# A fused attention and mixture-of-experts layer on one core: a shorter loop body in a branch that is not taken, and one unit's loads issued later

## The chip, the core and the metric

One Trainium2 chip, one core of it. The metric is device time in microseconds (us) from one launch. The engines are named as in the profile: PE (TensorE matmul), PEld (its weight load), DVE (VectorE), ACT (ScalarE), POOL (GpSimd) and SP (SyncE, which issues nearly all transfers). A "q" behind an engine's name is its sequencer or its queue of transfers.

## What is computed

The reference, cut to what matters (B = 4, T = 1024, C = 256, 16 heads of 16; all float32):

```
att = einsum('bhqd,bhkd->bhqk', q, k) / sqrt(D) + rel_bias      # causal mask, then softmax over keys
y   = einsum('bhqk,bhkd->bhqd', softmax(att), v) @ W_proj.T + b_proj
x   = layernorm(x + y)
e   = argmax(x @ gate_w.T)                                      # each token goes to one of 2 experts
out = layernorm(x + relu(x @ w1[e] + b1[e]) @ w2[e] + b2[e] + relu(x @ sw1 + sb1) @ sw2 + sb2)
```

The kernel does not subtract an exact row maximum before each exponential. It computes a bound (the "guard") from the norms of queries and keys and feeds its negative in as two extra rows of the query operand. Only if that bound is too loose (the flag `wide`) does it compute exact row maxima. With the inputs of this reference the flag is 0, so that part is built into the program but is skipped at run time.

## The kernel before, in words

Three stages run one after the other: `project_in` (queries, keys and values from x), `attend` (attention), `feed_forward` (projection, gate, experts, shared network). Between the first two stands `exact_maxima`, whose code on SP, PE and DVE lies inside an `If` on the flag `wide`. Each engine has its own instruction stream and the engines meet through semaphores only.

**The end of `project_in`.** DVE computes the flag and the guard value in a chain of one-element operations (L620 to L636). PE spreads the guard over the partitions (L742), ACT writes it to `neg_guard` (L528), and POOL fills `guard_fill` from it (L488, L490) and signals `ready.fill`. SP's stream at that place is the list that the change reorders. It stores tile 6's projected queries and keys to DRAM (`qk_d`, L412). It loads the second attention unit's stacks, which is `first_stack(1)`: eight transfers into `k_st` and `q_second` (L252 to L255), 1.5 MB together. It waits for `ready.fill`, writes the guard rows of all later units to DRAM (`guard_d`, L446 and L448), waits for those writes, loads the second unit's guard rows (L272), waits for `ready.decided`, and stores the last tile (L412).

**The branch.** On DVE the `If` stands at L801. Its body has a loop over batches (L810) and in it a loop over the two halves of the heads (L811), whose body is written out for 8 heads times 8 blocks of queries, 64 pairs of an addition (L822) and a maximum (L826). Behind the body come L836, which signals `ready.decided`, and the attention's code. PE's and SP's branches stand at L840 and L776.

**`attend`.** A unit is four heads of one batch, so there are 16 units. A unit has 9 steps times 2 pairs of heads, 18 in all. For each, PE computes scores into one of three slots of PSUM (L1157), DVE adds the bias in place for blocks near the diagonal (L1123), ACT takes the exponential (L1068 in the first unit, L1066 later) into `probs`, and PE multiplies by the values into `o_ps` (L1176). PE computes scores two steps ahead. Units take turns between two buffers: `q_first` for the first and third, `q_second` for the second and fourth. PE waits for a unit's ten loads before its first score (`st_ld`, L1146). SP loads the third unit once the last tile has been stored (L967) and PE has made all scores of the first unit (L933).

Of the kernel before, what the change touches and what calls it, by code (L numbers as in the profile page):

```python
# [14 lines left out]
ALU = mybir.AluOpType  # L15
ACT = mybir.ActivationFunctionType
AX = mybir.AxisListType

P = 128
B, T, C = 4, 1024, 256  # L20
H, D = 16, 16
HID = 1024
E = 2
KC = C // P
# [7 lines left out]
KB = T // P  # L32
BUCKETS = 32
WIN = 2 * P
# [212 lines left out]
def load_parts(sp, q_rows, k_rows, first, k_st, q_st, loaded):  # L247

    for side in range(2):
        at = ROWS_H * side  # L250
        heads = slice(first + side, first + side + UH - 1, 2)
        sp.dma_start(k_st[at:at + 2 * D].bitcast(F32), k_rows[0:2 * D, heads]).then_inc(loaded, 16)  # L252
        sp.dma_start(k_st[at + 2 * D:at + 3 * D].bitcast(F32), k_rows[0:D, heads]).then_inc(loaded, 16)
        sp.dma_start(q_st[at:at + D].bitcast(F32), q_rows[0:D, heads]).then_inc(loaded, 16)
        sp.dma_start(q_st[at + D:at + 3 * D].bitcast(F32), q_rows[0:2 * D, heads]).then_inc(loaded, 16)  # L255


def unit_rows(qk_d, b, g):

    rows = qk_d.rearrange("b c n (d h) t -> b c (n d) h t", d=D)  # L260
    q_rows = rows[bass.ds(b, 1), g // 2].rearrange("o r h t -> (o r) h t")
    k_rows = rows[bass.ds(b, 1), KC + g // 2].rearrange("o r h t -> (o r) h t")
    return q_rows, k_rows, UH * (g % 2)


def load_guard(sp, guard_d, b, g, q_st, loaded):

    rows = guard_d[bass.ds(b, 1)].rearrange("o g h t -> (o g) h t")
    for side in range(2):
        at = ROWS_H * side + STACK  # L270
        heads = slice(UH * g + side, UH * g + side + UH - 1, 2)
        sp.dma_start(q_st[at:at + GUARD].bitcast(F32), rows[:, heads]).then_inc(loaded, 16)  # L272
# [9 lines left out]
def overlay(nc, name, shape, dt, at):  # L282
    return nc.alloc_sbuf_tensor_at(name, shape, dt, offset=at)
# [21 lines left out]
def project_in(nc, keep, ready, slots, o_ps, ident, wp_hi, wp_lo, bp_row, v_all, shared_at, y_at, bias_t, wide, neg_guard, guard_fill, qk_d, guard_d, pad_row, rs_at,  # L305
# [3 lines left out]
    HG = H // KC  # L309
    with ExitStack() as ctx:  # L310
# [68 lines left out]
        def sync(sp):  # L379
# [47 lines left out]
            def first_stack(g):  # L427

                q_st = (q_first, q_second)[g]
                load_parts(sp, *unit_rows(qk_d, 0, g), k_st[:, g], q_st, st_ld[g])  # L430
                if g < AP_UNITS:
                    load_guard(sp, guard_d, 0, g, q_st, st_ld[g])
# [6 lines left out]
            sp.wait_ge(guard_out, 16)  # L439
            first_stack(0)  # L440
            body(B - 1, True, False)
            first_stack(1)
            sp.wait_ge(ready.fill, 2)
            for part in range(GUARD):
                src = guard_fill[:, part].bitcast(F32)
                sp.dma_start(guard_d[0, part, AP_UNITS * UH:H].rearrange("h t -> (h t)").rearrange("(p n) -> p n", p=P),  # L446
                             src[:, 0:(H - AP_UNITS * UH) * T // P]).then_inc(ready.guard_rows, 16)
                sp.dma_start(guard_d[1:B, part].rearrange("b h t -> b (h t)").rearrange("b (p n) -> p b n", p=P),  # L448
                             src.unsqueeze(1).to_broadcast([P, B - 1, P])).then_inc(ready.guard_rows, 16)
            sp.wait_ge(ready.guard_rows, 32 * GUARD)  # L450
            load_guard(sp, guard_d, 0, AP_UNITS, q_second, st_ld[AP_UNITS])
            sp.wait_ge(ready.decided, 1)
# [290 lines left out]


        return Stage(sync, gpsimd, scalar, vector, tensor)


def exact_maxima(nc, keep, ready, slots, o_ps, ident, bias_t, wide, qk_d, guard_d, q_first, q_second, st_ld, shared_at):


    HG = H // KC
    STEPS_C = HG * KB
    PARTS_DMAS = 8
    with ExitStack() as ctx:
        def sb(name, shape, dt=F32):
            return ctx.enter_context(nc.sbuf_tensor(name, shape, dt))

        def sem(name):
            return keep.enter_context(nc.semaphore(name))

        bias_q = overlay(nc, "bias_q", [P, H, WIN], F32, shared_at)
        q_all = overlay(nc, "q_all", [P, UH // 2, T], F32R, shared_at + 4 * H * WIN)
        k_all = overlay(nc, "k_all", [P, UH // 2, T], F32R, shared_at + 4 * H * WIN + 2 * UH * T)
        most = sb("most", [P, H * KB])
# [4 lines left out]
        added = sem("added"); maxed = sem("maxed"); most_ps = sem("most_ps"); neg_ok = sem("neg_ok")  # L769
# [29 lines left out]
        def vector(dve):  # L799
            dve.wait_ge(ready.wide, 1)  # L800
            with dve.If(dve.value_load(wide[:, :], min_val=0, max_val=1) != 0):  # L801
                dve.sem_inc(ready.decided, 1)
                dve.sem_inc(maxed, 2)
                dve.sem_inc(neg_ok, 1)
                for i in range(H // UH):
                    dve.wait_ge(turned, i + 1)
                    dve.tensor_copy(bias_q[:, UH * i:UH * i + UH, :],
                                    slots[:, i % 2].rearrange("p a (i x) -> p (a i) x", x=WIN)).then_inc(bias_q_ok, 1)
                dve.wait_ge(bias_q_ok, H // UH)
                with dve.Fori(0, B) as b:  # L810
                    with dve.Fori(0, KC) as c:  # L811
                        for h in range(HG):
                            for qb in range(KB):
                                k = KB * h + qb
                                n = STEPS_C * (KC * b + c) + k
                                row = slots[:, k % 2].rearrange("p a x -> p (a x)")
                                first = P * max(qb - 1, 0)
                                width = P * (qb + 1) - first
                                dve.wait_ge(scored, n + 2)
                                if k == 0:  # L820
                                    dve.wait_ge(neg_ok, b + 1)
                                dve.tensor_tensor(row[:, first:first + width], row[:, first:first + width],  # L822
                                                  bias_q[:, bass.ds(c * HG + h, 1), WIN - width:WIN].rearrange("p o x -> p (o x)"),
                                                  ALU.add).then_inc(added, 1)
                                dve.wait_ge(added, n + 1)
                                dve.tensor_reduce(most[:, bass.ds(c * STEPS_C + k, 1)], row[:, 0:P * (qb + 1)],  # L826
                                                  AX.X, ALU.max).then_inc(maxed, 1)
                    dve.wait_ge(most_ps, b + 1)
                    dve.tensor_scalar(neg[:, :], o_ps[:, 0, 0:P], -1.0, None, ALU.mult).then_inc(neg_ok, 1)
                    dve.wait_ge(neg_ok, b + 2)  # L830
                    dve.wait_ge(neg_out, 16 * GUARD * (b + 1))
                    dve.tensor_copy(neg_parts[:, 0], neg[:, :]).then_inc(split, 1)
                    dve.wait_ge(split, GUARD * b + 1)
                    dve.tensor_tensor(neg_parts[:, 1], neg[:, :], neg_parts[:, 0].bitcast(F32), ALU.subtract).then_inc(split, 1)
                dve.wait_ge(neg_out, 16 * GUARD * (B + 1))
            dve.sem_inc(ready.decided, 1)  # L836
# [40 lines left out]


        return Stage(sync, idle, idle, vector, tensor)


# [1249 lines left out]
```

## Time and profile before

| what | value |
|---|---|
| time, median of 3 runs | 818.05 us (817.14 to 818.75) |
| profiled execution, first to last instruction | 820.4 us |
| PE busy | 779.3 us, 95% of the span |
| ACT busy | 541.0 us, 66% |
| DVE busy | 509.0 us, 62% |
| POOL busy | 240.7 us, 29% |
| mean granted TensorE clock | 0.977 of full speed |

The busy share is an average over stages with different limits. Beside the span no other time of the profiled execution is given; it is 2.35 us above the median of the runs.

### The profile page before, as it was taken

To read this page: it belongs to the slowest core of one execution; us is meant where nothing else is said; L and a number is where in the kernel's file an instruction comes from. 1 tells how busy PE (TensorE), PEld (TensorE's weight loads), DVE (VectorE), ACT (ScalarE), POOL (GpSimd) and SP (SyncE) were. 2 spreads that over 40 slices of the span, in tenths; PEclk is the share of its full clock that TensorE was granted. 3 is DMA by queue.
4 is the path that set the end of the run, shared out by engine and by line. 5 is a ranking of instruction groups with operands and counts; after the bars stand their busy time and mean duration, and the time that the engine had idled before them with its cause. 6 is when DMAs were issued, how large, how long until landed. Compare 5 with 4: busy or idle time off the path is not lost.

```text
span 820.4 us, 16215 instructions
## 1 busy us (share of the span) xinstructions
PE 779.3 (95%) x6153; PEld 568.7 (69%) x6153; DVE 509.0 (62%) x1118; ACT 541.0 (66%) x700; POOL 240.7 (29%) x200
## 2 busy tenths in 40 slices
PE   7998849999999999999999999999999999999993
PEld 6886524444444444444889989889899998999992
DVE  4666426667666666765877788976634545554543
ACT  5666449999999999998455555544444455555442
POOL 6224310000020022036243545252532333223332
PEclk9999959999999999999999999999999999999997
DMA  8899975667797799891681211110475433444300
GB/s 238 231 287 279 216 173 93 93 120 120 118 179 129 122 156 177 136 174 20 119 285 59 66 65 54 53 45 34 145 264 198 161 123 140 168 176 165 141 27 29
DMA packets 57929, 114.41 MB, mean 139 GB/s; under 512 B 8019, under 2 KB 35064, under 8 KB 55544
## 3 DMA queue, kind: packets, MB, share of 16 engines
q1 hardware_dynamic: 53048, 100.60, 52.4%
q0 software_dynamic: 4800, 12.73, 4.4%
q8 instruction: 50, 0.82, 0.5%
q14 instruction: 31, 0.25, 0.1%
HBM read 57.75 MB, written 32.49 MB: 110 GB/s over the span
## 4 chain that ended last, share of the span: by engine, by line
PE 84%; DVE 6%; ACT 4%; issue 4%; DMA 1%; POOLq 0%; DVEq 0%; POOL 0%; ACTq 0%
PE slots L2043 20%; PE o_ps L1176 15%; PE slots L1157 14%; PE slots L2060 11%; PE o_ps L2060 10%; PE slots L708 6%; PE o_ps L670 2%; PE slots L1406 2%; ACT probs L1066 2%; DVE slots L1123 1%; PE slots L648 1%; PE slots L2025 1%; ACT probs L1068 1%; DVE junk L1798 1%; DVE other_row L1875 1%
## 5 line engine op out<-in xcount | busy, mean ns | idle before, releaser
L1066 ACT ACTIVATE probs<-slots 128x1024 f32<-128x1024 f32 x270 | 254.1, 1033 | 1.6
L1123 DVE TENSOR_TENSOR slots<-slots,bias_t 128x512 f32<-128x512 f32 (+1 forms) x288 | 163.6, 607 | 100.8 <-PE slots L1157 86.0
L1949 DVE TENSOR_TENSOR h_lo<-h_f,h_hi 128x512 fp32r<-128x512 f32 (+1 forms) x136 | 96.6, 712 | 107.6 <-PE o_ps L2060 70.1
L1176 PE MATMUL o_ps<-probs,v_st 128*32 128x384 f32 (+3 forms) x1920 | 155.5, 433 | 0.3 <-ACT probs L1066 0.3
L1767 ACT ACTIVATE h_f<-slots,b_cur 128x512 f32<-128x512 f32 (+1 forms) x72 | 47.9, 665 | 88.1 <-PE slots L2043 87.8
L1767 ACT ACTIVATE h_f<-slots,b_c 128x512 f32<-128x512 f32 x64 | 43.9, 687 | 67.6 <-PE slots L2043 65.6
L1771 ACT ACTIVATE h_hi<-h_f 128x512 fp32r<-128x512 f32 (+1 forms) x136 | 84.3, 620 | 4.3
L1157 PEld LDWEIGHTS slots<-q_first,k_st 50*128 50x128 f32 x480 | 38.7, 191 | 68.4 <-ACT probs L1066 37.2
L1157 PE MATMUL slots<-q_first,k_st 50*128 50x128 f32 (+3 forms) x480 | 70.0, 377 | 14.5 <-ACT probs L1068 12.5
L1176 PEld LDWEIGHTS o_ps<-probs,v_st 128*32 128x32 f32 x1920 | 46.5, 109 | 44.7 <-issue 28.0
L1157 PEld LDWEIGHTS slots<-q_second,k_st 50*128 50x128 f32 x480 | 37.5, 184 | 53.6 <-ACT probs L1066 42.2
L1157 PE MATMUL slots<-q_second,k_st 50*128 50x128 f32 (+3 forms) x480 | 68.7, 369 | 0.8
L1722 POOL DMA_INDIRECT out<-o_out,id_i x32 | 35.6, 1113 | 102.6 <-DVE o_out L1913 95.3
L1005 POOL COPY v_st<-v_all 128x512 f32<-128x512 f32 x16 | 9.7, 617 | 173.4 <-PE o_ps L1176 173.4
L1684 POOL DMA_INDIRECT xs_d<-x,slot_i x32 | 35.9, 1122 | 74.5 <-DVE slot_i L1829 67.2
L1684 POOL DMA_INDIRECT base_d<-base,slot_i x32 | 40.7, 1273 | 46.6 <-DVE base L1891 38.9
L2043 PE MATMUL slots<-x1t_lo,cur_hi 128*128 128x512 f32 (+1 forms) x144 | 43.3, 382 | 0.0
L2043 PE MATMUL slots<-x1t_hi,cur_lo 128*128 128x512 f32 (+1 forms) x144 | 43.3, 382 | 0.0
L2043 PE MATMUL slots<-x1t_hi,cur_hi 128*128 128x512 f32 (+1 forms) x144 | 43.2, 381 | 0.0
L2043 PE MATMUL slots<-x1t_hi,shared_hi 128*128 128x512 f32 x128 | 41.4, 404 | 1.2 <-ACT x1t_hi L1336 1.2
L2060 PE MATMUL slots<-experts_hi,h_hi 128*128 x144 | 41.3, 287 | 0.2
L2043 PE MATMUL slots<-x1t_lo,shared_hi 128*128 128x512 f32 x128 | 40.7, 399 | 0.2 <-DVE x1t_lo L1398 0.2
(243 smaller groups left out, 1709.3 us busy)
## 6 DMA issues: line engine op xcount, KB each, us to landing
qk_d<-parts SPq DMA_DIRECT2D x32, 512.0 KB, 8.3
cur_hi<-experts_hi SPq DMA_DIRECT2D x9, 1024.0 KB, 4.8
cur_lo<-experts_lo SPq DMA_DIRECT2D x9, 1024.0 KB, 6.9
k_st<-qk_d SPq DMA_DIRECT2D x32, 256.0 KB
xs_sb<-xs_d SPq DMA_DIRECT2D x8, 528.0 KB, 4.7
x_in<-L_attn_x SPq DMA_DIRECT2D x8, 512.0 KB, 7.8
k_st<-qk_d SPq DMA_DIRECT2D x32, 128.0 KB
q_first<-qk_d SPq DMA_DIRECT2D x16, 256.0 KB
```

The costliest lines, as they stand in the source:

```text
L708: ins = pe.matmul(slots[:, 1 + c // 2, c % 2], wq[w][:, kc, P * c:P * c + P], xt[a][:, t, kc, :], start=(i == 0 and kc == 0), stop=(i == 2 ...
L1066: nc.scalar.activation(dst, src, ACT.Exp).then_inc(exped, 1)
L1123: ins = dve.tensor_tensor(tile, tile, bias_t[:, h0:h0 + 2, first:first + w], ALU.add)
L1157: ins = pe.matmul(slots[:, k % SLOTS, h, col:col + w], k_st[at:at + KROWS, buf, pair, P * j:P * j + P], q_st[buf][at:at + KROWS, pair, q0: ...
L1176: ins = pe.matmul(o_ps[32 * j2:32 * j2 + 2 * D, half, q:q + w], v_st[:, g, j, j2, :], probs[:, (k + j2 // 2) % PBUFS, j2 % 2, col:col + w] ...
L1684: pool.indirect_dma_start(rows[:, :], bass.IndirectOffsetOnAxis(slot_i[:, t % 2, k:k + 1], 0), src[:, k, :], None).then_inc(done, 16)
L1722: pool.indirect_dma_start(out_rows[:, :], bass.IndirectOffsetOnAxis(id_i[:, j % 2, k:k + 1], 0), (o_out if j < EXP_TILES - 1 else y2)[:, k ...
L1767: nc.scalar.activation(h_f[:, q % 2, 0:w], l1_bank[q % 2][:, 0:w], ACT.Relu, bias=bias).then_inc(hf_ok, 1)
L1771: nc.scalar.activation(h_hi[:, n % 3, 0:w], h_f[:, q % 2, 0:w], ACT.Copy).then_inc(hh_ok, 1)
L1949: dve.tensor_tensor(h_lo[:, n % 3, 0:w], h_f[:, q % 2, 0:w], h_hi[:, n % 3, 0:w].bitcast(F32), ALU.subtract).then_inc(hl_ok, 1)
L2043: ins = pe.matmul(l1_bank[q % 2][:, 0:P * blocks(u)], w1_of(u, w)[:, kc, P * q:P * q + P], (xt_hi, xt_lo)[a][:, kc, 0:P * blocks(u)], star ...
L2060: ins = pe.matmul(acc_bank[k], (h_hi, h_lo)[a][:, n % 3, P * k:P * k + P], w2_chunk(u, w, q, e), start=(q == 0 and i == 0), stop=(q == HC ...
```

## The change

Two places of the program are rewritten, and nothing that is computed changes.

First, in the part of `exact_maxima` that DVE skips, the two nested loops (two halves of the heads, and eight heads written out in each) become one loop over all 16 heads. The body is then written out for one head: 8 pairs of addition and maximum in place of 64. Second, in SP's stream of `project_in`, `first_stack(1)` is moved from before the wait for `ready.fill` to behind the four writes of the guard rows.

```diff
             first_stack(0)
             body(B - 1, True, False)
-            first_stack(1)
             sp.wait_ge(ready.fill, 2)
             for part in range(GUARD):
...
                 sp.dma_start(guard_d[1:B, part].rearrange("b h t -> b (h t)").rearrange("b (p n) -> p b n", p=P),
                              src.unsqueeze(1).to_broadcast([P, B - 1, P])).then_inc(ready.guard_rows, 16)
+            first_stack(1)
             sp.wait_ge(ready.guard_rows, 32 * GUARD)
             load_guard(sp, guard_d, 0, AP_UNITS, q_second, st_ld[AP_UNITS])
             sp.wait_ge(ready.decided, 1)
...
                 with dve.Fori(0, B) as b:
-                    with dve.Fori(0, KC) as c:
-                        for h in range(HG):
-                            for qb in range(KB):
-                                k = KB * h + qb
-                                n = STEPS_C * (KC * b + c) + k
-                                row = slots[:, k % 2].rearrange("p a x -> p (a x)")
...
+                    with dve.Fori(0, H) as h:
+                        for qb in range(KB):
+                            n = H * KB * b + KB * h + qb
+                            row = slots[:, qb % 2].rearrange("p a x -> p (a x)")
...
+                            dve.tensor_reduce(most[:, bass.ds(KB * h + qb, 1)], row[:, 0:P * (qb + 1)],
+                                              AX.X, ALU.max).then_inc(maxed, 1)
```

On DVE, at the branch around the exact maxima, the rows of the instruction stream before are these (each with its number in the stream; L801 is the `If`, L1123 the first bias addition of the attention):

```order
75 L801 TENSOR_LOAD wide
76 L801 ISA x2
77 L801 COMPARE_AND_BRANCH
78 L807 COPY bias_q<-slots 128x1024 x4
...
363 L834 TENSOR_TENSOR neg_parts<-neg,neg_parts 128x128
364 L810 REGISTER_ALU
365 L810 COMPARE_AND_BRANCH
366 L801 UNCONDITIONAL_BRANCH
367 L1123 TENSOR_TENSOR slots<-slots,bias_t 128x2x128 x2
```

The same place of DVE's stream in the changed kernel (L1123 has become L1121):

```order
75 L801 TENSOR_LOAD wide
76 L801 ISA x2
77 L801 COMPARE_AND_BRANCH
78 L807 COPY bias_q<-slots 128x1024 x4
...
125 L832 TENSOR_TENSOR neg_parts<-neg,neg_parts 128x128
126 L810 REGISTER_ALU
127 L810 COMPARE_AND_BRANCH
128 L801 UNCONDITIONAL_BRANCH
129 L1121 TENSOR_TENSOR slots<-slots,bias_t 128x2x128 x2
```

The branch keeps its place, and the instruction that it lands on moves from row 367 to row 129: 289 rows are jumped over before, 51 after. DVE's whole stream shrinks from 883 rows to 645, and everything behind the branch lies 238 rows nearer the start.

On SP, at the end of `project_in`, the rows before (tile 6's stores, then the second unit's stacks, the guard rows, and the last tile's stores):

```order
L412 DMA qk_d<-parts 128x2x512 x4
L252 DMA k_st<-qk_d 32x2x1024
...
L255 DMA q_second<-qk_d 32x2x1024
L446 DMA guard_d<-guard_fill 128x96
L448 DMA guard_d<-guard_fill 128x3x128
L446 DMA guard_d<-guard_fill 128x96
L448 DMA guard_d<-guard_fill 128x3x128
L272 DMA q_second<-guard_d 2x2x1024 x2
L412 DMA qk_d<-parts 128x2x512 x4
```

And the same place of SP's stream in the changed kernel (L446 and L448 have become L445 and L447):

```order
L412 DMA qk_d<-parts 128x2x512 x4
L445 DMA guard_d<-guard_fill 128x96
L447 DMA guard_d<-guard_fill 128x3x128
L445 DMA guard_d<-guard_fill 128x96
L447 DMA guard_d<-guard_fill 128x3x128
L252 DMA k_st<-qk_d 32x2x1024
...
L255 DMA q_second<-qk_d 32x2x1024
L272 DMA q_second<-guard_d 2x2x1024 x2
L412 DMA qk_d<-parts 128x2x512 x4
```

The eight stack loads (the "..." stands for six of them) have changed places with the four writes of guard rows. The loads of the second unit's guard rows and the last tile's stores stay behind both.

## Rows read from the trace of the kernel before

**Rows 1.** The page's head, and busy time, share of span, instructions of PE.

```profile
span 820.4 us, 16215 instructions
...
PE 779.3 (95%) x6153; PEld 568.7 (69%) x6153; DVE 509.0 (62%) x1118; ACT 541.0 (66%) x700; POOL 240.7 (29%) x200
```

**Rows 2.** Stretches: PE, PEld, DVE, ACT, POOL busy (x), PEclk, DMA share, GB/s.

```profile
98.00:100.50 2.50, 1.42 (x9) 0.85 (x8) 0.02 (x1) 1.20 (x3) 1.70 (x4) 1.00 1.19 235
100.50:112.50 12.00, 0.00 (x0) 0.00 (x0) 1.36 (x3) 1.09 (x2) 4.14 (x6) 0.50 1.00 132
112.50:120.00 7.50, 7.11 (x34) 2.61 (x34) 2.86 (x5) 6.19 (x8) 0.00 (x0) 0.50 0.68 248
120.00:122.00 2.00, 2.00 (x28) 1.31 (x24) 0.87 (x2) 1.10 (x2) 0.00 (x0) 0.73 0.42 159
134.00:151.00 17.00, 16.85 (x184) 7.61 (x180) 11.30 (x21) 16.87 (x19) 0.62 (x1) 1.00 0.68 111
```

**Rows 3.** Chain that ended last, 98 to 132 us: start, us, what.

```profile
98.97 11.73 issue
110.70 0.02 DVEq L836
...
110.88 0.45 DVE slots L1123
...
111.41 3.13 ACT probs L1068 x3
```

**Rows 4.** Transfer queues, whole span: packets, MB, share of 16 engines.

```profile
q8 instruction: 50, 0.82, 0.5%
q14 instruction: 31, 0.25, 0.1%
```

**Rows 5.** The same queues, 99 to 107 us: the data queue q1.

```profile
q1 hardware_dynamic: 429, 1.17, 107.7%
```

**Rows 6.** The same queues, 107 to 109 us: the instruction queue q14.

```profile
q14 instruction: 1, 0.01, 2.0%
```

**Rows 7.** Timeline of PE, 97 to 99.6 us, first score: start, us.

```profile
99.45 0.50 PE L1157 MATMUL slots<-q_first,k_st 50*128 50x512 f32 x2 [1.00 <-ACT neg_guard L528]
```

**Rows 8.** Timeline of PE, 97 to 150 us: second and third unit's first scores.

```profile
130.55 1.02 PE L1157 MATMUL slots<-q_second,k_st 50*128 50x512 f32 x4
...
147.83 0.84 PE L1157 MATMUL slots<-q_first,k_st 50*128 50x512 f32 x4
```

**Rows 9.** Timeline of ACT, 95 to 133 us: first unit's 18 exponentials.

```profile
111.41 6.14 ACT L1068 ACTIVATE probs<-slots,neg_guard 128x1024 f32<-128x1024 f32 x6 [11.83 <-DVE slots L1123]
118.85 2.12 ACT L1068 ACTIVATE probs<-slots,neg_guard 128x1024 f32<-128x1024 f32 x2 [1.31 <-DVE slots L1123]
121.87 10.15 ACT L1068 ACTIVATE probs<-slots,neg_guard 128x1024 f32<-128x1024 f32 x10 [0.90 <-DVE slots L1123]
```

**Rows 10.** Timeline of SP's issues, 84 to 136 us: start, us.

```profile
89.17 0.50 SPq L252 DMA_DIRECT2D k_st<-qk_d  x1
...
99.52 0.37 SPq L446 DMA_DIRECT2D guard_d<-guard_fill  x1
...
100.94 0.47 SPq L448 DMA_DIRECT2D guard_d<-guard_fill  x1
113.61 0.58 SPq L272 DMA_DIRECT2D q_second<-guard_d  x2
114.30 3.32 SPq L412 DMA_DIRECT2D qk_d<-parts  x4
129.72 0.35 SPq L252 DMA_DIRECT2D k_st<-qk_d  x1
```

**Rows 11.** Stretches again, by transfers (columns as in Rows 2).

```profile
114.50:121.50 7.00, 6.91 (x40) 2.89 (x44) 2.53 (x5) 5.17 (x6) 0.00 (x0) 0.53 0.83 303
...
129.70:142.70 13.00, 12.83 (x138) 5.54 (x133) 7.95 (x15) 12.88 (x15) 0.62 (x1) 1.00 0.88 146
142.70:147.00 4.30, 4.30 (x48) 2.07 (x52) 3.56 (x7) 4.29 (x5) 0.00 (x0) 1.00 0.02 5
```

More of the change, by code:

```diff
@@ L810, in vector @@
                 with dve.Fori(0, B) as b:
-                    with dve.Fori(0, KC) as c:
-                        for h in range(HG):
-                            for qb in range(KB):
-                                k = KB * h + qb
-                                n = STEPS_C * (KC * b + c) + k
-                                row = slots[:, k % 2].rearrange("p a x -> p (a x)")
[L817 to L827, printed above, removed]
+                    with dve.Fori(0, H) as h:
+                        for qb in range(KB):
+                            n = H * KB * b + KB * h + qb
+                            row = slots[:, qb % 2].rearrange("p a x -> p (a x)")
+                            first = P * max(qb - 1, 0)
+                            width = P * (qb + 1) - first
+                            dve.wait_ge(scored, n + 2)
+                            if qb == 0:
+                                dve.wait_ge(neg_ok, b + 1)
+                            dve.tensor_tensor(row[:, first:first + width], row[:, first:first + width],
+                                              bias_q[:, bass.ds(h, 1), WIN - width:WIN].rearrange("p o x -> p (o x)"),
+                                              ALU.add).then_inc(added, 1)
+                            dve.wait_ge(added, n + 1)
+                            dve.tensor_reduce(most[:, bass.ds(KB * h + qb, 1)], row[:, 0:P * (qb + 1)],
+                                              AX.X, ALU.max).then_inc(maxed, 1)
                     dve.wait_ge(most_ps, b + 1)
```

## Prediction

> **What bounds the kernel now.** I read the page first: PE is busy 95% of the span [rows 1], so over the whole kernel only idle time of PE, or slow PE, is to be won. Then I looked for where it idles. The stretches show one hole: from 100.5 to 112.5 us PE executes nothing at all, at the seam between the projections and the attention, and the granted clock of TensorE falls there from 1.00 to 0.50, its lower level of 1.2 GHz, at which PE still works until about 121 us [rows 2]. In steady attention (134 to 151 us) ACT is busy 16.87 of 17.00 us [rows 2], so a unit lasts 17 us there, and from then on what is late at the seam is late to the end.
>
> The chain of waits says who makes the hole. From 98.97 to 110.70 us it stands on "issue", 11.73 us in which the engine waits for nothing that the profile names, between DVE's branch over the exact maxima (L801) and the first instruction behind it (L836) [rows 3]. Only 0.18 us later DVE adds the first bias, and 0.53 us after that ACT starts the first exponential, at 111.41 us [rows 3]. PE's first score had been begun at 99.45 and was there at 99.95 us [rows 7]. So the data were ready 10.9 us before DVE took them.
>
> What DVE waits for is code, by this working. Queue q14 carries packets of kind instruction, 31 of them with 0.25 MB, about 8 KB each; q8 has 50 with 0.82 MB, 16 KB each [rows 4]. PE and its weight loads are 2 x 6153 of the 16215 instructions [rows 1]. 12306 / 50 = 246 per packet of q8, and the other four engines' 3909 / 31 = 126 per packet of q14: both near 65 bytes an instruction, so q8 feeds PE and q14 the others. After the jump at 98.97 us there is no packet on q14 until 107, and one between 107 and 109 us [rows 5, 6], just ahead of DVE's return. All that time the data queue q1 fills the 16 transfer engines (107.7% of them from 99 to 107 us) [rows 5]. That backlog is tile 6's stores and, behind them, the second unit's stacks, issued from 89.17 us [rows 10].
>
> **The change part by part.** *The loop.* The jump goes over 289 rows before and over 51 after, as the order shows. At about 126 instructions a packet that is 2.3 packets before and 0.4 after. If DVE holds the packet that it runs in and the next one, the target before lies outside and the target after inside, wherever in its packet the branch stands. PE speaks for jumps within held code being cheap: its own branch skips some 160 rows, and its first score still starts 1.00 us after PE's last work, with ACT's guard as releaser [rows 7]. So I cost the fetch at nothing after the change: DVE is past the branch at 98.97 + 0.18 = 99.15 us and waits for the first score at 99.95. The bounds: nothing from above; from below, a fetch that stays takes at least what the trace shows from packet to return, some 2 us (110.70 minus a packet seen before 109) [rows 3, 6], and up to 4 us with its request.
>
> *The gain at the seam.* First addition at about 100.0 us, first exponential at 100.0 + 0.53 = 100.5. It stood at 111.41, so 10.9 us are won. If DVE could only begin when all first three scores are made it would be some 0.5 us less.
>
> *The clock.* Between the first unit's 18 exponentials ACT waits 1.31 and 0.90 us, 2.2 us together, 6 and 10 us after it began, while PE is at the lower level [rows 9, 2]; a steady unit has no such waits [rows 2]. After the change PE pauses for about 2 us in place of 12. But the clock was already down right behind 100.5 us, when PE had hardly stopped [rows 2], so it may fall all the same and come back after the 8 to 9 us of work that it took before. Bounds 0 and 2.2 us; I take half, 1.1, since nothing in the rows decides.
>
> *The moved loads.* SP issues the guard rows from 99.52 to 101.41 us [rows 10]. The eight stack issues follow at once, 101.4 to 105.3 at the pitch of 0.47 us that they have before, and then the guard rows of the second unit and the last tile's stores. Eight SP issues lose their old place in a wait for `ready.fill` that SP sat out anyway, so the move costs SP nothing. What counts is landing. The third unit's loads show the time alone: issued from 129.72 us, the engines are at 0.88 until 142.7 and at 0.02 after [rows 10, 11], 13.0 us with the first unit's outputs (1/7 of the packets) among them, so 11 to 13 without and with. The guard writes ahead add 1 to 2 us. The second unit's stacks land at 101.4 + 12 + 1.5 = 115, bounds 113.5 and 119 (if the guard writes take the 7 us more that mixing with stacks may cost them). PE needs them at 130.55 before [rows 8], 12.0 us earlier after: 118.5, or 117.4 if the clock's 2.2 are won. That is 2.4 to 3.5 us in time at the middle value.
>
> *What is late next.* The last tile's stores queue behind the stacks. Before they fill 114.5 to 121.5 us [rows 11], and after, from 115, they end at about 121. SP may not load the third unit until they land, so it issues at 121 to 122 and not 8 us after them as now (129.72) [rows 10]. With 11 to 13 us it lands at 132 to 135. PE needs it at 147.83 - 12.0 = 135.8 [rows 8]. So both loads arrive, with 1 to 4 us to spare, less slack than the 5 us of today. I cost them at nothing, with 3 us as the far bound. From the fourth unit on the order is as before.
>
> *Sum.* 10.9 + 1.1 = 12.0 us off the profiled span: 820.4 to 808.4. The runs' median is 818.05, 2.35 below the span; the same 12.0 us off it gives 806.0.
>
> **A rule to weigh.** Rows 6 show 8 KB a packet for DVE's queue. The Trainium skill ("Runtime: NRT & Kernel Launch", Instruction fetch mechanics) says that engines refill in 16 KiB blocks of 256 instructions, hold two, and stall on a taken branch to a target outside them. By its block size 289 rows would reach one block on, or two; where it is one, the target was already held, the 11.73 us were no such fetch and the shorter loop would be worth nothing. The trace agrees with the kind of stall and not with the block size, so I go by 126 instructions; the page's size is one more reason for the next case.
>
> **The rivals.** *The fetch stays* (the loop doesn't do what it is for: the target isn't held all the same, or any taken branch of DVE fetches). For it: no row shows a short jump of DVE. Against it: PE's cheap jump [rows 7]. Even then the moved loads help: the data queue has only guard rows at that time, and the stacks are issued 2.4 us after the jump. DVE returns at 101 to 103 us rather than 99.15; the first addition is at 101.2 to 103.2, 1.2 to 3.2 us later than forecast: 807.2 to 809.2.
>
> *The stacks come late.* The second unit at the far bound of 119 us costs 0.5 to 1.6 us, or the third unit, behind stacks and stores in one queue, up to 3: 806.5 to 809. For it: the engines are full from 101 to 135 us without a break. Against it: the middle values above.
>
> *Slower.* The fetch stays and is also caught by the moved loads. Its request at 98.97 precedes the first stack issue by 2.4 us; but if it is served only when q1 runs dry, as now, it waits for guard rows and stacks, to 115 us, and DVE comes back at about 115 + 2 = 117, 6.3 us later than 110.70: 824.3. It decides where DVE returns after 110.7 us. Against it: q1 must hold 10 us of work at the moment of the request, and at 99 us it holds the end of tile 6's stores.
>
> **How the numbers follow.** Forecast 0.69; the fetch stays, short, 0.14; stacks late 0.11; slower 0.02; no difference (a gap of another cause, which neither edit touches) 0.04. The predicted time is 806.0. Forecast alone: 804.9 to 807.6, from the clock's bounds of 1.1 us either way and 0.5 for the score; the two faster rivals reach 809.2. The range is 803.9 to 809.3, which takes in the 0.8 us by which the runs of before differ from their median. A difference of 0.2%, 1.6 us, is about what a measurement of this kernel can tell from no change. All three cases that end between 804 and 809.2 are faster by more: 0.94 faster, 0.04 same, 0.02 slower.
>
> **What would show it.** Right: no "issue" wait on DVE at the branch, its first addition at about 100 us and the first exponential at 100.5; no hole of PE over 3 us between 100 and 113; the first scores from `q_second` at 117.5 to 118.5, with ACT as releaser and not a load; the clock row telling which end of the 1.1 holds. Wrong: an "issue" wait of 2 us or more with a q14 packet at its end (the first rival); PE waiting for a load of `k_st` or a queue of transfers at 117 or 135 us (the second).

## The result, and the profile after

| kernel | median | lowest to highest | runs |
|---|---|---|---|
| before, same chip | 818.4 us | 817.14 to 820.93 | 4 |
| changed | 810.25 us | 808.95 to 814.13 | 4 |

The ratio of the times is 0.9898 [0.9877, 0.9919]: faster, by 8.15 us between the medians. The forecast of 806.0 us was 4.25 too low, and its range ended at 809.3. Yet the profiled execution of the changed kernel has a span of 808.6 us, against the 808.4 that the sum gave for the span. The section behind the experiments takes that apart. One later execution of the kernel before, of 1211.03 us at a granted clock of 0.556, is left out of every ratio and count below.

The page's head after the change: PE does the same work in a shorter span (compare [rows 1]).

```profile
span 808.6 us, 16215 instructions
...
PE 777.2 (96%) x6153; PEld 567.4 (70%) x6153; DVE 510.3 (63%) x1118; ACT 541.2 (67%) x700; POOL 240.9 (30%) x200
```

The chain that ended last, 98 to 104 us (start, us, what), answers to [rows 3].

```profile
98.47 0.18 ACT neg_guard L528
98.65 0.79 issue
99.44 0.52 PE slots L1155 x2
100.06 0.44 DVE slots L1121
100.58 3.13 ACT probs L1066 x3
```

The 11.73 us on "issue" at DVE's branch are gone. What is left of that kind is 0.79 us, in which PE comes from its last projection to its first score, as it did before at 99.45 [rows 7]. DVE takes the score 0.10 us after it is there, and the first exponential starts at 100.58, where it stood at 111.41 [rows 3].

The stretches around the seam, where the projections end and the attention begins (columns as in [rows 2]):

```profile
98.00:101.00 3.00, 1.40 (x9) 0.85 (x8) 0.94 (x4) 1.59 (x4) 2.21 (x4) 1.00 0.12 35
101.30:108.00 6.70, 5.93 (x30) 2.61 (x34) 2.39 (x6) 5.42 (x6) 3.33 (x5) 0.50 0.86 147
108.20:120.00 11.80, 11.45 (x124) 5.07 (x120) 7.67 (x14) 11.80 (x12) 0.00 (x0) 1.00 1.02 250
```

The hole of PE is gone. From 101.3 us the clock is still at its lower level, 0.50, but for 7 us and not for some 20. The DMA share from 98 to 101 us is 0.12, where it was 1.19 from 98 to 100.5 [rows 2]: with the stacks behind the guard rows, the transfer engines stand nearly empty just when the engines jump. The queues from 99 to 101 us (packets, MB, share of 16 engines) show what uses that gap:

```profile
q1 hardware_dynamic: 137, 0.05, 9.0%
...
q8 instruction: 1, 0.02, 2.9%
```

A 16 KB packet on q8, PE's code, comes at 100.0 us. In the kernel before it came at 108.6. The experiments turn on this row.

The timeline of ACT, first unit (start, us, operation, the idle time before it), answers to [rows 9]:

```profile
100.58 6.14 ACT L1066 ACTIVATE probs<-slots,neg_guard 128x1024 f32<-128x1024 f32 x6 [1.02 <-DVE slots L1121]
108.03 12.23 ACT L1066 ACTIVATE probs<-slots,neg_guard 128x1024 f32<-128x1024 f32 x12 [1.31 <-DVE slots L1121]
```

Of the two waits inside the unit, the one of 1.31 us has stayed and the one of 0.90 has gone; the clock is back at 1.00 by then.

The timelines of PE (first scores of the second and third units, compare [rows 8]) and of SP (compare [rows 10]):

```profile
118.79 1.02 PE L1155 MATMUL slots<-q_second,k_st 50*128 50x512 f32 x4
...
136.09 0.85 PE L1155 MATMUL slots<-q_first,k_st 50*128 50x512 f32 x4
```

```profile
102.38 0.52 SPq L252 DMA_DIRECT2D k_st<-qk_d  x1
...
106.50 0.59 SPq L272 DMA_DIRECT2D q_second<-guard_d  x2
107.20 3.24 SPq L412 DMA_DIRECT2D qk_d<-parts  x4
121.81 0.35 SPq L252 DMA_DIRECT2D k_st<-qk_d  x1
```

No load releases these two scores, and the third unit begins 147.83 - 136.09 = 11.74 us earlier. SP goes back to the third unit at 121.81, inside the 121 to 122 of the prediction. Further on there is one new wait, between the ninth and the tenth unit (waits, 228 to 262 us: us in total, times, longest):

```profile
PEld slots L1155 <- DMA q_second<-guard_d: 1.3, 1, 1.3
PE slots L1155 <- DMA q_second<-guard_d: 0.8, 1, 0.8
ACT probs L1064 <- DVE slots L1121: 0.7, 1, 0.7
```

### The profile page after: what moved, and what is told of

Read it like the earlier page. It is cut to its first block, busy times and chain, and to the rows that moved or that the text cites. A ratio compares the mean times of both kernels' runs of the same rounds, so it can differ in the third digit from the quotient of the medians.

```text
span 808.6 us, 16215 instructions
## 1 busy us (share of the span) xinstructions
PE 777.2 (96%) x6153; PEld 567.4 (70%) x6153; DVE 510.3 (63%) x1118; ACT 541.2 (67%) x700; POOL 240.9 (30%) x200
## 4 chain that ended last, share of the span: by engine, by line
PE 84%; DVE 6%; ACT 4%; DMA 2%; issue 2%; SPq 0%; POOLq 0%; POOL 0%; ACTq 0%; DVEq 0%
PE slots L2041 20%; PE o_ps L1174 14%; PE slots L1155 13%; PE slots L2058 11%; PE o_ps L2058 10%; PE slots L708 6%; PE o_ps L670 2%; PE slots L1404 2%; ACT probs L1064 2%; DMA q_second<-guard_d 2%; DVE slots L1121 1%; DVE junk L1796 1%; PE slots L648 1%; PE slots L2023 1%; ACT probs L1066 1%
## 5 line engine op out<-in xcount | busy, mean ns | idle before, releaser
L1121 DVE TENSOR_TENSOR slots<-slots,bias_t 128x512 f32<-128x512 f32 (+1 forms) x288 | 163.5, 607 | 89.8 <-PE slots L1155 88.0
L2058 PE MATMUL slots<-experts_hi,h_lo 128*128 x144 | 40.5, 281 | 0.0
```

What stands on the lines that cost most here:

```text
L1121: ins = dve.tensor_tensor(tile, tile, bias_t[:, h0:h0 + 2, first:first + w], ALU.add)
L2058: ins = pe.matmul(acc_bank[k], (h_hi, h_lo)[a][:, n % 3, P * k:P * k + P], w2_chunk(u, w, q, e), start=(q == 0 and i == 0), stop=(q == HC ...
```

## The experiments

In the expectations A is the account that the prediction or the runs so far support, and the other letters are the rivals that each of them states. The ratio of a run is to the kernel before on the same chip.

### The same two kernels again

> The kernel before, unchanged, to see what a single profile of it is worth. Its profiled execution spanned 820.4 us, while its runs took 818.4 us; the changed kernel's runs take 1.7 us more than their spans. Theory A (the wait of DVE at the branch differs from execution to execution, and the profiled one caught a long one): another profile spans about 816 to 818 us and shows a wait of 7 to 10 us where the first showed 11.73; the five runs' spans differ by some us. Rival B (the wait is always 11.7 us, and the changed kernel's runs lose elsewhere what they win): the wait is again 11.5 to 12 us and the span again about 820.

> The changed kernel, unchanged, beside the others on one chip. Both theories: first exponential at 100.5 to 100.6 us; time 808 to 812 us, 0.986 to 0.992 of before. Theory A (the loads of stacks are now and then late by chance, as at the tenth unit of the first profile, 0.84 us): the place of that wait differs or it is not there. Rival B (the moved loads put the tenth unit's guard rows late): the same wait of about 0.8 us at the same unit.

> The kernel before once more, for its profile alone. Two profiles of it show the first exponential at 111.41 and 108.27 us and spans of 820.4 and 816.5. Theory A (the wait at the branch differs with the time at which the code packet gets through the backlog): the code packet of DVE lies 8 to 10 us after the branch, the first exponential follows it by 3 us, between 107 and 112 us, and the span follows the first exponential one to one, within 1.5 us. Rival B (the spans differ for another reason): the span does not follow the first exponential.

The kernel before took 820.51 us, median of 12 runs (818.09 to 821.98), ratio 1.0009 [0.999, 1.0029], and in its further profile 819.45. The changed one took 810.08, median of 10 (809.36 to 816.63), ratio 0.99 [0.9871, 0.9929]. Waits of DVE at the seam in the three profiles of before, the first one, e1 and e8 (this view counts from DVE's last operation; the chain of [rows 3] counts from the branch and has 11.73 us for the first):

```profile
DVE slots L1123 <- issue: 12.9, 1, 12.9
```

```profile
DVE slots L1123 <- issue: 10.6, 1, 10.6
```

```profile
DVE slots L1123 <- issue: 12.2, 1, 12.2
```

The wait differs by 2.3 us between executions, and the span goes with it:

| profile | wait on "issue" | first exponential | span | span less first exponential |
|---|---|---|---|---|
| before | 12.9 us | 111.41 | 820.4 | 709.0 |
| e8, before again | 12.2 | 110.10 | 817.7 | 707.6 |
| e1, before again | 10.6 | 108.27 | 816.5 | 708.2 |
| changed | none | 100.58 | 808.6 | 708.0 |

So what is late at the first exponential is late at the end, within 1.5 us, as the prediction had it. ACT's second wait inside the first unit, 0.90 us in the first profile of before [rows 9], is 0.40 in e1, and e8 has none. In the second profile of the changed kernel the ninth unit lasts 18.09 us, and 17.87 in the first; a unit elsewhere takes about 17. The wait for the tenth unit's guard rows comes back at the same place, so it belongs to the kernel and not to one execution.

### One part of the change alone

The loop alone is the diff of DVE without that of SP, the loads alone that of SP without that of DVE.

> The loop over the heads alone; the second unit's loads stay in their old place. Theory A (the wait at the branch is a code fetch, and the target after the change is held): DVE's first bias addition at about 100.0 us, no wait for issue, first exponential at 100.5, and the time of the changed kernel within 0.2%, 809 to 811 us; the moved loads add nothing. Rival B (DVE still fetches, and only the moved loads make the fetch short): the wait stays at 8 to 12 us, first exponential at 108 to 111, time about 817 to 819.

> The moved loads alone; the long loop stays. Theory A (the fetch waits behind the data that fill the transfer engines): the fetch stays, but the engines are nearly free at 99 us, so the wait at the branch is 2 to 4 us, the first bias addition at 101.2 to 103.2, first exponential at 101.7 to 103.7, and the time 811 to 814. Rival B (a fetch on its own queue is not held up by another queue's data, and the wait has another cause): the wait stays at 8 to 12 us, time 817 to 819.

**The loop alone** took 817.37 us, median of 12 (813.82 to 825.34), ratio 0.9987 [0.9956, 1.0018]: no measurable gain. DVE did not fetch, for its first addition is at 99.75 us. But the chain that ended last stops again, on another engine:

```profile
104.35 1.86 PE o_ps L1174 x6
106.21 4.05 issue
110.26 1.86 PE o_ps L1174 x2
```

PE has made 22 matmuls of the attention (its timeline shows 16 of scores and 6 into `o_ps`; the 28 in the expectation of e5 is a miscount) and then stands for 4.05 us with nothing to wait for. ACT waits 7.21 us in the middle of the first unit, which lasts 25.5 us. The queues of this run, first 99 to 106 us, then 106 to 108:

```profile
q1 hardware_dynamic: 461, 1.35, 107.9%
```

```profile
q8 instruction: 1, 0.02, 4.7%
```

There is no packet of PE's code up to 106 us, and one between 106 and 108, ahead of PE's going on at 110.26. Until then q1 moved 1.35 MB in 461 packets, 2.9 KB each; the 280 packets beside PE's are of 1.0 KB. The code comes when the stacks' long packets end, with q1 still full. So PE too needs code at the seam. Neither account had this; the time is the one that B forecast, but DVE's wait, by which B had it, is gone. In the kernel before, PE's need lies under DVE's longer wait.

**The loads alone** took 813.09 us, median of 8 (811.44 to 814.18), ratio 0.9927 [0.9903, 0.9951]. The chain, then the queues from 99 to 101 us:

```profile
98.94 2.77 issue
...
101.90 0.44 DVE slots L1123
...
102.43 3.13 ACT probs L1068 x3
```

```profile
q1 hardware_dynamic: 135, 0.05, 8.6%
...
q8 instruction: 1, 0.02, 4.4%
q14 instruction: 1, 0.01, 1.6%
```

DVE still fetches, but with q1 at 8.6% the packet is there at 99.9 us, and the chain has 2.77 us where it had 11.73 behind a q1 of 107.7% [rows 3, 5]. In the view of waits that is 3.9 us against 10.6 to 12.9. Most of the old wait was the queue of stacks, not the fetch.

### PE's branch made short

In place of moving the loads, PE's skipped loop is shortened too. The new body holds one stack of four heads:

```diff
-                    with pe.Fori(0, KC) as c:
-                        for h in range(HG):
-                            if h % UH == 0:
-                                pe.wait_ge(all_ld, 16 * PARTS_DMAS * (2 * (KC * b + c) + h // UH + 1))
+                    with pe.Fori(0, H // UH) as u:
+                        pe.wait_ge(all_ld, 16 * PARTS_DMAS * ((H // UH) * b + u + 1))
+                        for h in range(UH):
...
-                                pe.wait_ge(maxed, STEPS_C * (KC * b + c) + k + 1)
+                                pe.wait_ge(maxed, UH * KB * ((H // UH) * b + u) + k + 1)
```

In the order of the instructions PE's jump then goes over 88 rows and not 165. Three kernels have it: e5 with the loop of DVE and the loads unmoved, e6 with the whole change, e11 with neither.

> The loop over the heads on DVE, loads in their old place as in the run of the loop alone, and PE's own skipped part shortened too: four heads written out in a loop over four groups in place of eight in a loop over two halves, so that PE jumps over 88 rows and not 165. In the run of the loop alone PE ran out of code after 28 matmuls of the attention and stood 4.05 us, because its code packet came at 106.7 us, behind the stacks. Theory A (PE's jump uses up the code that it holds ahead; a shorter jump leaves some): the stall of PE is gone, the first unit lasts 18.4 to 19.6 us in place of 25.5, the time is 808 to 812 us with the loads unmoved. Rival B (PE fetches and stalls at any jump, or stalls for data): a stall of 3 to 5 us stays in the first unit, time 815 to 819.

> The changed kernel (short loop on DVE, moved loads) with PE's skipped part shortened as well. Theory A (in the changed kernel PE's code comes in time because the moved loads leave the transfer engines free at 99 us): nothing changes, first unit 19.4 to 19.5 us, time within 0.2% of the changed kernel, 809 to 811. Rival B (PE still loses time to code in the changed kernel): first unit under 19 us and the time 0.5 to 1.5 us less.

> The kernel before with PE's skipped part shortened and nothing else (DVE's long loop, loads in their old place). Theory A (PE's own fetch was hidden behind DVE's wait in the kernel before): DVE's wait of 9 to 12 us stays, first exponential at 108 to 112 us, time within 0.2% of before. Rival B (PE's fetch cost the kernel before time too): 2 us or more less than before.

**e5** took 810.3 us, median of 4 (807.79 to 811.15), ratio 0.9885 [0.9866, 0.9904], its profile with a span of 806.1 the shortest of all profiles. A part of that is not the edit's: the spreading of the guard (L742) starts at 97.19 us in this execution, and at 98.06 in the profile of the changed kernel. There is no stall of PE. Its code packet is late as ever, between 105 and 106 us; with the target 77 rows nearer, PE does not stop before it comes. **e6** took 811.89 (6 runs, 810.13 to 815.81), ratio 0.991 [0.9888, 0.9933], which is 0.9 us above the range of A, but not less than the change: with the loads moved, no gain of PE's short jump shows. **e11** took 820.23 (10 runs, 818.47 to 821.27), ratio 0.9995 [0.9979, 1.001]. PE's short jump alone gives nothing, as DVE's wait stands over it:

```profile
DVE slots L1122 <- issue: 10.9, 1, 10.9
```

Together with e2 and e3 they say what the seam needs. Two engines need code there. Either both jumps are short, and the stacks may fill the queue; or the stacks are issued later, and both fetches are quick. One short jump with the queue full leaves the other engine's stall.

### How far DVE may jump

The changed kernel with instructions added to the part that DVE skips (`for _ in range(125): dve.memset(most[:, :], 0.0)` behind the loop over the batches, then 175 of them). The jump goes over 176 and 226 rows.

> The changed kernel with 125 more instructions in the skipped body on DVE, so that the branch jumps over 176 in place of 51 and its target lies about 1.4 code packets on. Theory A (DVE holds the packet that it runs in and the next; packets of q14 come when DVE is about 64 instructions past a multiple of 128, so what is held at the branch reaches some 215 instructions on): no fetch at the branch, first bias addition at 100.0 to 100.1 us. Rival B (only a target in the same packet is free): a packet on q14 at about 100 us and the first addition at 101.5 to 103.

> The same with 175 more instructions: a jump over 226. Theory A: just outside what is held, so a packet on q14 at about 100 us, and the first bias addition at 101.5 to 103, as with the long loop and moved loads (101.9). Rival B (DVE holds two blocks of 256 instructions, so only jumps beyond 256 or more fetch): no fetch, first addition at 100.0 to 100.1 us.

DVE's first additions, 176 rows and then 226 (timeline; in brackets the idle time before):

```profile
99.94 1.36 DVE L1123 TENSOR_TENSOR slots<-slots,bias_t 128x256 f32<-128x256 f32 x3 [2.05 <-PE slots L1157]
```

```profile
103.12 1.36 DVE L1123 TENSOR_TENSOR slots<-slots,bias_t 128x256 f32<-128x256 f32 x3 [4.04 <-issue]
```

At 176 rows DVE waits for the score alone. At 226 it waits 4.04 us for nothing, with a packet on q14 at 101.0 us. The reach of a free jump from this branch thus ends between 176 and 226 rows, and the 289 of before lie outside it. That is where A in e9 put it, some 215, but the place of a packet's coming from which A worked this out, 64 instructions past a multiple of 128, no view here shows. A packet on q14 does come at 100.0 us at 176 rows, but DVE's addition has begun by then, so nothing waits for it. That run took 815.07 us with a span of 813.3, one run: guard rows come late again. The second unit lasts 18.08 us, as the third unit's guard rows hold PE up for 1.0 us, and units eight to ten last 18.2 to 19.4. So a clean seam does not by itself make a fast run.

### The new wait at the tenth unit

In the changed kernel, the guard rows of a unit are now loaded ahead of its stacks:

```diff
+                load_guard(sp, guard_d, b, g, q_st[buf], st_ld[buf])
                 load_parts(sp, *unit_rows(qk_d, b, g), k_st[:, buf], q_st[buf], st_ld[buf])
-                load_guard(sp, guard_d, b, g, q_st[buf], st_ld[buf])
```

> The changed kernel, and in the loads of later units the two small transfers of guard rows are issued before the eight of the stacks. In both profiles of the changed kernel PE waits for the guard rows of the tenth unit, which makes its predecessor last 17.9 and 18.1 us in place of 17.0. Theory A (those rows are late because they stand last behind 1.5 MB): no unit after the first lasts over 17.1 us, span 0.8 to 1.1 us less (about 807.7), time 808.5 to 810. Rival B (the transfer engines are late as a whole at that place, with the stacks): the wait moves to the stacks and stays at about 1 us; time as the changed kernel's, 809.5 to 811.

It took 810.73 us (6 runs, 809.73 to 813.1), ratio 0.9888 [0.987, 0.9907], no better. The eighth and ninth units last 17.69 and 17.78 us, and PE now waits for the stacks:

```profile
PEld slots L1155 <- DMA q_first<-qk_d: 1.6, 2, 1.1
```

The order of the ten loads is not the cause; whatever comes last of them is late. From 205 to 260 us q1 takes 96.6% to 100.2% of the transfer engines in the five profiles that have the moved loads and a first exponential before 101 us (the change twice, e6, e7 and e9), and 87.1% to 91.7% in the four with DVE's old wait and the loads unmoved. All five have late loads there (e6 the least, 0.6 us before PE's weight loads). The loads of the shared network's weights (`load_shared`) fall into that stretch. In e13 they are issued behind the next unit's loads:

```diff
-                if 1 <= b <= 2:
-                    load_shared(b - 1)
...
+                if 1 <= b <= 2:
+                    load_shared(b - 1)
```

> The changed kernel with the 1 MB loads of shared weights (in the second and third batch) issued behind the next unit's stacks and not ahead of them. In the profiles of the changed kernel the transfer engines are full from 205 to 260 us, PE waits there for guard rows of the ninth to twelfth unit (0.84 and 1.08 us in two profiles, 4.8 in that of the jump over 176 rows), and its runs spread upwards, to 816 us. Theory A (these late loads are the upward spread, and the shared weights ahead of the tenth unit's stacks cause them): no unit after the first lasts over 17.1 us, the median is 0.5 to 1.5 us less (809), and no run is over 812. Rival B (the engines' pace differs from execution to execution, whatever stands ahead): the waits and the spread stay, median 810 to 811.

It took 810.65 us (4 runs, 809.3 to 811.17), ratio 0.9876 [0.9859, 0.9893], in a comparison in which before took 821.35 and the change itself did not run. q1 is at 89.7% from 205 to 260 us, no later unit exceeds 17.1 us and no run 812. That is what transfers as the cause would give, but the median is not lower than that of the change (A had 809), the interval overlaps, and four runs do not settle it.

### The clock

In e12, on e5, PE is given work where it would pause: 8 matmuls behind the guard's spreading (L742) and 10 behind the first three scores, from a weight tile into `o_ps`, whose results nothing uses. e14 is e12 with the shared weights later.

```diff
+            pe.wait_ge(v_ev, TILES - 1)
+            for _ in range(8):
+                pe.matmul(o_ps[:, 0, 0:C], wp_hi[:, 0, 0:P], wp_hi[:, 0, :], start=True, stop=True)
...
+                if k == SLOTS:
+                    for _ in range(10):
+                        pe.matmul(o_ps[:, 0, 0:C], tile.wp_hi[:, 0, 0:P], tile.wp_hi[:, 0, :], start=True, stop=True)
```

> The run with both short branches and the loads in their old place, and 18 matmuls more on PE whose results are not used: 8 between the spreading of the guard and the first score, 10 after the first three scores, where PE otherwise pauses twice for 1.0 to 1.3 us. Theory A (the granted clock falls behind 100 us because PE pauses at the seam): the clock stays at 1.00 through the first unit, ACT's wait of 1.31 us there is gone, the first unit lasts 18.4 us in place of 19.4, span about 1 us less than without, 805. Rival B (the clock falls for what PE does there, not for its pauses): it falls all the same behind 100 us, and the first unit lasts 19.4 us.

> Both short branches, loads in their old place, no pause of PE at the seam, and the shared weights' loads issued behind the next stacks: the version that the experiments point to. Theory A: first exponential at 100.0 to 100.8 us, first unit 18.0 us, no later unit over 17.1, span 805 to 807.5, median 807 to 809.5 and no run over 812. Rival B (the spread to 819 us of the run without PE's pause has another cause): median 810 to 812 and runs up to 817 again.

Stretches of e5 and then of e12 (columns as in [rows 2]), and ACT's first unit in e12:

```profile
99.90:106.60 6.70, 5.41 (x26) 2.42 (x26) 2.39 (x6) 5.96 (x6) 3.87 (x6) 0.50 1.06 157
```

```profile
101.00:108.00 7.00, 5.93 (x48) 2.80 (x47) 3.53 (x7) 7.00 (x8) 3.71 (x6) 1.00 1.02 162
```

```profile
100.73 18.20 ACT L1068 ACTIVATE probs<-slots,neg_guard 128x1024 f32<-128x1024 f32 x18 [1.08 <-DVE slots L1123]
```

PE pauses for 0.51 and 0.45 us around its first scores and not for 1.00 and 1.34, the clock stays at 1.00 (2.4 GHz), ACT has none of its two waits, and the first unit lasts 17.96 us in place of 19.43: 1.5 us won in that unit. The span of the profile is 807.4 us all the same and not the 805 of A: the guard's spreading starts at 98.13 us, 0.94 later than in e5. e12's median is 811.88 us (8 runs, 807.98 to 818.99), ratio 0.9906 [0.9873, 0.9938]; its runs spread over 11 us, and what the seam gives is lost in that. e14 took 809.79 (4 runs, 807.33 to 810.32), ratio 0.9854 [0.9831, 0.9876]. It is the lowest ratio measured, with an interval that ends just below that of the change, [0.9877, 0.9919], from another comparison. A did not hold in full: in e14's profile, with a span of 808.6, the second unit lasts 17.69 us, since the third unit's guard rows hold PE up for 0.6 us, although the second unit's loads are in their old place.

## Why the prediction was right and wrong

**What held.** The 10.9 us at the seam were 111.41 - 100.58 = 10.83. The half of the clock's 2.2 us, taken as 1.1 since nothing decided it, was one of the two waits, 0.90. But the further profiles of before have 0.40 and none in its place, so these 0.90 us belong to the profiled execution and not to the change alone. "820.4 to 808.4" stands against 808.6 measured. That they agree within 0.2 us is partly luck: the ninth unit lost 0.84 us that the sum did not have, and from the last exponential to the end the profiled execution took 432.1 us after and 432.9 before, in stages that neither edit touches. "If DVE holds the packet that it runs in and the next one, the target before lies outside and the target after inside" was put to the test by e9 and e10: a reach of 176 to 226 rows is more than one packet of 126 and less than two, as it would be from a branch that stands within the first. On the rule that was weighed, the Trainium skill ("Runtime: NRT & Kernel Launch", Instruction fetch mechanics) gives blocks of 256 instructions, two held (the 8 KB a packet that the prediction sets against it follow from rows 4, not from rows 6). By it a jump over 226 rows lands at the latest in the next block, and would be free. e10's 4.04 us disagree for DVE; PE's packets of 246 [rows 4] fit the page's size.

**The step that failed** is the last line of the sum: "The runs' median is 818.05, 2.35 below the span; the same 12.0 us off it gives 806.0". It joins two numbers of different executions. Wherever this study has both for one execution, the time is 1.67 to 1.83 us above the span (810.34 and 808.6 for the changed kernel, 818.26 and 816.5 for e1). So the profiled execution of before took about 820.4 + 1.7 = 822.1 us, 4 us more than the median beside which it was shown. It was a long one: in the comparisons of the experiments the kernel before ran 65 times, on three chips, with spans of 814.4 to 822.1 and a median of 818.4, and 8 of the 65 reach 820.4. The 12.0 us were rightly the saving of that execution, and they were taken off a median to which it did not belong. Put the other way, span after plus 1.74, the same sum gives 808.4 + 1.74 = 810.1 us, and 810.25 was measured (810.34 in the profiled execution). The prediction saw the 2.35 us and read nothing from them; but a time below the span of the same program says that the two are not one execution.

The saving of a typical execution is smaller. DVE's wait was 10.6 to 12.9 us in three profiles of before, and the prediction had the longest. Between the median spans, 818.4 (65 executions) and 808.5 (14 of the changed kernel), it is 9.9 us, and 8.15 us between the two medians of four runs in the result. The range was narrow besides. It "takes in the 0.8 us" of the runs' scatter, but 809.3 is only 0.1 above the 809.2 of its slower rivals; with 0.8 it would have ended at 810.0, still below 810.25.

**A reason that failed without cost.** The forecast gave the moved loads no gain of their own: "the move costs SP nothing. What counts is landing." Only its first rival let them help. They are worth most of the change: loads alone 0.9927, loop alone 0.9987, both 0.9898. They clear the transfer engines for PE's code. The prediction took PE's branch as proof that jumps within held code are cheap, "its first score still starts 1.00 us after PE's last work". The row [rows 7] is right, but it shows the first score alone. What was not followed is how far PE comes on the code it holds: 22 matmuls in e2, then 4.05 us of nothing. In the trace of before PE's packet between 107 and 109 us lies under DVE's wait, and no row gives it a price. The total came out right because the change does both.

**The rivals.** "The fetch stays" fell at the branch (no "issue" wait of DVE, no q14 packet from 99 to 107 us), and so did "slower"; e3 is what the former would have looked like, 2.77 us, in its range of 1.2 to 3.2 for the first addition (101.90 against 100.0). "The stacks come late" fell at the places named: the second unit's first score is at 118.79 with no load as releaser, a little behind the 117.5 to 118.5 of the forecast. The slack at the third unit is small, though: its guard rows are late in e9 and in e14. Loads are late at the tenth unit in both profiles of the change, where the prediction said "as before" and the new wait costs 0.8 us of PE. "No difference" fell with the interval of the ratio.

**Open** is why the runs of the changed kernel reach up to 814.1 and 816.6 us while most lie within 1 us of 808.4 in span. Of the eight profiles with a first exponential before 101 us and the shared weights in their old place, late loads at the ninth to eleventh unit are in all five with the moved loads and in one of three without. They are in none of the four with DVE's old wait, not in e3 and e10, which have the moved loads but start later, and not in e13 and e14, where the shared weights are out of the way. That points to the transfers, and to the moved loads as a part of it, but rests on one profile each and on four runs each of e13 and e14; it is not shown.

## What to carry to other kernels

Before a saving read from one profiled execution is taken off a median, put that execution among the runs: compare like with like, span with span, and give the saving the spread that the removed wait itself has. At a jump, look at the code of every engine that jumps there, not only of the one that the chain of waits names, and follow the others until they have used up what they hold. Where code has to be fetched, what stands in the data queues at that moment sets the price, and issuing bulk loads some microseconds later can be worth more than shortening the code.

## What the runs showed of the hardware

- **Code waits behind data.** A jump of DVE that had to fetch held it up for 3.9 and 4.0 us with nearly free transfer engines (e3 and e10, q1 at 8.6% around the packet), and for 10.6 to 12.9 us behind a full q1 (before, e1, e8, e11), all by the view of waits, though instruction packets have a queue of their own. The Trainium skill ("DMA: Bandwidth & Descriptors", Queues, rings and completion order) lets each transfer engine take turns between queues, and go through a whole packet, typically some 9 to 17 descriptors and at most 64, before it turns. From 99 to 107 us 429 packets of q1 went by [rows 5], 27 for each of the 16 engines, ahead of one of q14. If those are descriptors, that is 1.6 to 3 of the page's typical packets, but less than one of its longest; no row tells how the descriptors were packed or when the request reached the engines, so whether the rule explains the wait stays open. The wait is not over only when q1 runs dry, as the prediction thought of its slower rival: in before, e2 and e5 the packet came with q1 at 90% or more, once its packets had gone from 2.7 KB and more to about 1 KB.
- **A jump can stall later than at its target.** PE started its first score on time and stopped 7 us later, at 106.21 us, where its next code packet came at 106.73 (e2); that the code it held had ended is the reading that fits e5, where a shorter jump has no stall.
- **The clock fell behind PE's short pauses at the seam.** It stood at 0.50 for 7 us in the changed kernel and in e5, where PE pauses for 1.0 and 1.34 us around its first scores, and stayed at 1.00 in e12 and e14, where extra matmuls fill these pauses and the longest that is left in e12 is 0.51 us.
